# Handing a fused cross-attention kernel its context with the features on the partitions, and regrouping its PSUM banks

## The reference, cut to what matters

```python
# x: 16 batches of 128 tokens x 512 features; ctx_1024: 16 x 2048 x 512
# cross-attention with 16 query heads of 32 and ONE key/value head of 32
K, V = ctx @ Wk + bk, ctx @ Wv + bv                      # 2048 x 32 each
x = x + softmax((layernorm(x) @ Wq + bq) K^T / sqrt(32)) V @ Wo + bo
x = x + memory_attention(layernorm(x))                   # 4 heads of 128, a triangular inverse per head
x = x + moe(layernorm(x))                                # 16 experts, one per token, 128 tokens each
```

## Time and profile before

| what | value |
|---|---|
| time, median of 3 runs | 2176.65 us (2176.55 to 2177.91) |
| span of the profiled execution, first to last instruction | 2171.3 us |
| around the span, against the median | 5.35 us |
| PE busy, over the span | 2095.7 us (97%) |
| PE weight loads busy | 1421.6 us (65%) |
| POOL busy | 1635.7 us (75%) |
| DVE busy / ACT busy | 1272.3 us (59%) / 1220.7 us (56%) |
| transposes at L412 from the context in w_first | 992, mean 276 ns, together 151.5 us |
| mean granted TensorE clock | 0.986 |

### The profile page before, as it was taken

One profiled execution on the slowest core, in us unless ns is written; L12 is line 12 of the kernel. 1 busy time (PEld: TensorE's weight loads), 2 busy tenths in 40 slices (PEclk: granted clock), 3 DMA queues, 4 the chain that ended last, 5 costly groups with the idle time before them and its releaser, 6 DMA issues. The chain is left out here.

```text
span 2171.3 us, 35745 instructions
## 1 busy us (share of the span) xinstructions
PE 2095.7 (97%) x12908; PEld 1421.6 (65%) x12908; DVE 1272.3 (59%) x2226; ACT 1220.7 (56%) x2277; POOL 1635.7 (75%) x1387
## 2 busy tenths in 40 slices
PE   7879999999999999999999999999989999999999
PEld 5436565656565656666565656565645789999998
DVE  5656767676666666676767676766664433333332
ACT  3756575666666566666665666666655233433333
POOL 0778888888888888888888888889798145555555
PEclk8989999999999999999999999999999999999999
DMA  4752121212212121212131212112200089999994
GB/s 159 242 113 90 48 74 45 73 52 66 75 48 74 45 73 53 74 44 82 39 97 43 74 43 74 59 57 71 79 15 11 12 313 357 363 352 359 360 348 177
DMA packets 107055, 262.31 MB, mean 121 GB/s; under 512 B 8960, under 2 KB 34304, under 8 KB 98688
## 3 DMA queue, kind: packets, MB, share of 16 engines
q1 hardware_dynamic: 96912, 234.92, 31.6%
q10 hardware_dynamic: 6384, 14.62, 2.3%
q0 software_dynamic: 3584, 10.49, 1.2%
HBM read 223.67 MB, written 25.72 MB: 115 GB/s over the span
## 5 line engine op out<-in xcount | busy, mean ns | idle before, releaser
L1094 POOL TENSOR_TENSOR psum<-psum,weights 128x512 f32<-128x512 f32 x896 | 1152.6, 1286 | 163.4 <-ACT weights L702 60.5
L880 DVE TENSOR_REDUCE mpart<-bank 128x1 f32<-128x512 f32 x1024 | 680.4, 684 | 308.9 <-PE bank L447 300.0
L702 ACT ACTIVATE weights<-bank 128x512 f32<-128x512 f32 x1024 | 597.0, 599 | 324.1 <-PE bank L460 313.3
L460 PE MATMUL bank<-qT,kT 97*128 97x512 f32 x1024 | 482.8, 477 | 10.0 <-DMA qT<-mrow 6.5
L447 PE MATMUL bank<-kT,qT 96*128 96x512 f32 x1024 | 450.0, 451 | 9.6 <-DVE mpart L880 6.8
L447 PEld LDWEIGHTS bank<-kT,qT 96*128 96x128 f32 x1024 | 196.9, 192 | 141.2 <-issue 87.4
L1346 POOL TENSOR_TENSOR w2l<-w,w2h 128x1024 fp32r<-128x1024 f32 x64 | 202.9, 3171 | 75.8 <-PE ebank L1259 54.5
L460 PEld LDWEIGHTS bank<-qT,kT 97*128 97x128 f32 x1024 | 195.7, 193 | 89.4 <-issue 49.2
L472 PE MATMUL bank<-weights,v 128*32 128x512 f32 x2048 | 251.3, 609 | 0.0
L737 ACT COPY w_first<-bank 128x512 f32<-128x512 f32 x248 | 144.7, 584 | 67.6 <-PE bank L412 64.6
L1289 ACT ACTIVATE hh<-ebank 128x512 fp32r<-128x512 f32 x64 | 38.2, 597 | 224.6 <-PE ebank L1243 224.6
(11 more groups left out here) (174 smaller groups left out, 3019.3 us busy)
## 6 DMA issues: line engine op xcount, KB each, us to landing
w<-in_w SPq DMA_DIRECT2D x48, 2048.0 KB, 19.9
w_first<-in_ctx SPq DMA_DIRECT2D x62, 1024.0 KB, 5.2
w_first<-in_w SPq DMA_DIRECT2D x16, 2048.0 KB, 12.2
dispatched<-route ACTq DMA_DIRECT2D x17, 513.0 KB, 8.5
dis<-dispatched SPq DMA_DIRECT2D x16, 513.0 KB, 3.5
qT<-qh SPq DMA_DIRECT2D x128, 64.0 KB, 3.4
qT<-qs SPq DMA_DIRECT2D x64, 64.0 KB, 2.1
xr<-in_x SPq DMA_DIRECT2D x16, 256.0 KB, 2.7
```

Of the source, the lines that this page charges most:

```text
L460: e.matmul(B_BANK[u % 2][:], kT[b % 2][0:3 * HD + 1, k * P:(k + 1) * P], qT[b % 2][0:3 * HD + 1, g * 512:(g + 1) * 512], start=True, stop= ...
L702: e.activation(p[n % NP], B_BANK[u % 2][:], ACT.Exp).then_inc(p_act.sem, 1)
L880: e.tensor_reduce(mpart[g % 2][:, 4 * (n % 4) + n // 4:4 * (n % 4) + n // 4 + 1], max_bank(b, g, n)[:], AX.X, ALU.max).then_inc(max_dve.se ...
L1094: e.tensor_tensor(acc[:], first, p[(UNITS * b + u) % NP], ALU.add).then_inc(psum_pool.sem, 1)
```

## The change

The host now lays the context out as [batch, part, feature within a plane, plane, token], so that each part lands in SBUF as `kv` wants it. The 16 tile transposes of each batch, the copies behind them (ACT's, and DVE's for batch 0) and their waits are gone. All four parts of `cxT` have a place of their own, and the part of the batch after next is loaded four ticks after the `kv` step that frees its place. The bank `T_BANK` becomes the third bank of maxima; the turned `x` and the turned values go to `KV_BANK`. The other weights (`Wq`, `Wo` and so on) are laid out by planes too, which makes each partition's piece of a load contiguous. Preparation of batch 0 is pulled together.

```diff
-WARM = {-1: 14, 14: 4}
+WARM = {-1: 14, 10: 4}
...
-Prep = namedtuple("Prep", "norm xn xnt qproj qsend tiles kv vt")
-STEADY = Prep(norm=-32, xn=-29, xnt=-27, qproj=[24, 26, 27, 29], qsend=52,
-              tiles=[9, 12, 13, 15, 18, 24, 27, 32, 35, 39, 44, 50, 53, 54, 60, 69],
-              kv=[18, 37, 58, 74], vt=[42, 79])
+STEADY = Prep(norm=-32, xn=-29, xnt=-27, qproj=[24, 26, 27, 29], qsend=52, kv=[18, 37, 58, 74], vt=[42, 79])
...
-FIRST = Prep(norm=6, xn=9, xnt=12, qproj=[14, 15, 16, 17], qsend=22,
-             tiles=[2, 3, 4, 5, 6, 7, 8, 9, 19, 20, 21, 22, 28, 29, 30, 31], kv=[10, 23, 33, 38], vt=[27, 43])
-LOAD_AT = [13, 45, 71, 80]
+FIRST = Prep(norm=4, xn=6, xnt=8, qproj=[11, 12, 13, 14], qsend=19, kv=[7, 10, 16, 18], vt=[20, 22])
+LOAD_AFTER, W1_AT = 4, 80
...
-FIRST_MAX, FIRST_TURN = [35, 35, 36, 36, 40, 40, 41, 41, 42, 42, 43, 43, 44, 44, 45, 45], 47
+FIRST_MAX, FIRST_TURN = [24 + n // 2 for n in range(KB)], 33
...
-        A_BANK, B_BANK, PV_BANK, T_BANK, KV_BANK, P_BANK = bank[0:2], bank[2:4], bank[4], bank[5], bank[6], bank[7]
+        A_BANK, B_BANK, PV_BANK, KV_BANK, P_BANK = [bank[0], bank[1], bank[5]], bank[2:4], bank[4], bank[6], bank[7]
...
+            + [(TICKS * (b - 1) + prep(b).xnt, b, ("x", 0)) for b in range(B)]
+            + [(TICKS * (b - 1) + t, b, ("v", m)) for b in range(B) for m, t in enumerate(prep(b).vt)]
...
-            return [*A_BANK, P_BANK][n % 3] if b == g == 0 else A_BANK[(17 * g + n) % 2]
+            return A_BANK[(17 * (HG * b + g) + n) % 3]
+
+        def max_read(b, g, n):
+
+            before_g, before_n = divmod(17 * (HG * b + g) + n - 3, 17)
+            if before_g < 0:
+                return None
+            return max_dve.at(0, KB * before_g + before_n) if before_n < KB else mrow_act.at(0, before_g)
...
-                e.dma_start(chunk(b, c), T["ctx"][b].rearrange("(p c k) d -> c p k d", c=4, k=4)[c]).then_inc(
-                    ctx_in[c].sem, 16)
+                if b:
+                    e.wait_ge(*kv_pe.at(b - 1, c))
+                e.dma_start(cxT[c], T["ctx"][b, c]).then_inc(ctx_in[c].sem, 16)
...
-                if t in prep(b).tiles:
-                    k = prep(b).tiles.index(t)
-                    c, kk = divmod(k, 4)
-                    if kk == 0:
-                        e.wait_ge(*ctx_in[c].at(b))
-                    read = turn_read(b, ("t", k))
-                    if read is not None:
-                        e.wait_ge(*read)
-                    transposes(turn_bank(b, ("t", k)), lambda j: chunk(b, c)[:, kk, j * P:(j + 1) * P]).then_inc(t_pe.sem, 1)
                 if t in prep(b).kv:
                     c = prep(b).kv.index(t)
-                    e.wait_ge(*copied(b, 4 * c + 3))
+                    e.wait_ge(*ctx_in[c].at(b))
...
+    ctx = np.ascontiguousarray(g["ctx_1024"].reshape(B, 4, S // 4, DC, P).transpose(0, 1, 4, 3, 2))
```

More of the change, by code:

```diff
@@ L152, in attention @@
         pad_dve, pad_pool = sb("pad_dve", [P, 1]), sb("pad_pool", [P, 1])
-        cx = [w1_first[:, c, :].rearrange("p (k d) -> p k d", k=4) for c in range(2)]
-        cxT = [w1_first[:, 2 + c, :].rearrange("p (c t) -> p c t", c=DC) for c in range(2)]
-        def chunk(b, c):
-            return weights[:, 2048 * (c - 2):2048 * (c - 1)].rearrange("p (k d) -> p k d", k=4) if b == 0 and c >= 2 else cx[c % 2]
+        cxT = [w1_first[:, c, :].rearrange("p (c t) -> p c t", c=DC) for c in range(4)]
         kvlow, kvs = sb("kvlow", [P, 512]), [sb(f"kvs{i}", [P, 512]) for i in range(2)]
@@ L237, in level @@
             return (b, lv) if b < LAST else (b, 4 * lv + part)
-        uses = sorted((TICKS * b + t, b, use) for b in range(B) for t, use in
-                      [(prep(b).xnt, ("x", 0))] + [(t, ("t", k)) for k, t in enumerate(prep(b).tiles)]
-                      + [(t, ("v", c)) for c, t in enumerate(prep(b).vt)])
-        turns, holds, first_uses = {}, {}, 0
-        for _, b, use in uses:
-            place = 0
-            if b == 0:
-                place, first_uses = first_uses % 4, first_uses + 1
-            turns[b, use] = place, holds.get(place)
-            holds[place] = b, use
-        def copied(b, k):
-            if b:
-                return cxT_act.at(b, k - KB // 2)
-            return cxT_dve.at(0, k // 2) if k % 2 else cxT_act.at(0, k // 2)
-        def turn_bank(b, use):
-            return [T_BANK, *B_BANK, PV_BANK][turns[b, use][0]]
-        def turn_read(b, use):
-            if turns[b, use][1] is None:
-                return None
-            before_b, (kind, i) = turns[b, use][1]
-            if kind == "x":
-                return xnT_act.at(before_b)
-            return copied(before_b, i) if kind == "t" else v_act.at(before_b, i)
         kv_uses = [(b, use) for _, b, use in sorted(
@@ L311, in banks_of @@
         def banks_of(b):
-            return [P_BANK] if b < LAST else [P_BANK, KV_BANK, T_BANK, PV_BANK]
+            return [P_BANK] if b < LAST else [P_BANK, KV_BANK, A_BANK[2], PV_BANK]
         def att_done(b, h):
@@ L499, in prepare @@
                     e.wait_ge(*xn_act.at(b))
-                    read = turn_read(b, ("x", 0))
+                    read = kv_read(b, ("x", 0))
                     if read is not None:
                         e.wait_ge(*read)
-                    transposes(turn_bank(b, ("x", 0)), lambda j: xin[:, j * P:(j + 1) * P]).then_inc(xnT_pe.sem, 1)
+                    transposes(KV_BANK, lambda j: xin[:, j * P:(j + 1) * P]).then_inc(xnT_pe.sem, 1)
                 if t in prep(b).qproj:
@@ L537, in prepare @@
                         rows = slice(64 * (j % 2), 64 * (j % 2) + 2 * HD)
-                        ins = e.matmul(KV_BANK[rows, :], wkv[:, j, :], cxT[c % 2][:, j, :], start=j < 2, stop=j >= 2)
+                        ins = e.matmul(KV_BANK[rows, :], wkv[:, j, :], cxT[c][:, j, :], start=j < 2, stop=j >= 2)
                     ins.then_inc(kv_pe.sem, 1)
@@ L542, in prepare @@
                     e.wait_ge(*kvs_dve.at(b, 2 * m + 1))
-                    e.wait_ge(*turn_read(b, ("v", m)))
-                    transposes(turn_bank(b, ("v", m)), lambda j: kvs[m][:, j * P:(j + 1) * P]).then_inc(vT_pe.sem, 1)
+                    e.wait_ge(*kv_read(b, ("v", m)))
+                    transposes(KV_BANK, lambda j: kvs[m][:, j * P:(j + 1) * P]).then_inc(vT_pe.sem, 1)
             def finish(b, t):
@@ L724, in prepare @@
                     e.wait_ge(*xnT_pe.at(b))
-                    e.copy(xnT[:].rearrange("p c t -> p (c t)"), turn_bank(b, ("x", 0))[:]).then_inc(xnT_act.sem, 1)
+                    e.copy(xnT[:].rearrange("p c t -> p (c t)"), KV_BANK[:]).then_inc(xnT_act.sem, 1)
                 if t == prep(b).qproj[3] + 2:
```

74 lines of the change are left out of this document (23 added, 51 removed).

## The result

| | before | after |
|---|---|---|
| time, median | 2177.28 us (2176.55 to 2178.03, 4 runs) | 2141.61 us (2140.20 to 2145.51, 4 runs) |
| ratio, 95% interval | | 0.984 (0.9828 to 0.9853) |
| profiled execution: span | 2171.3 us | 2140.6 us (time 2142.43 us) |
| granted clock, whole span | 0.986 | 0.979 |

The change makes the kernel 35.7 us faster, 1.6%. So the time of before moves by some 4 us from one comparison to the next, and the gain is 31 to 36 us. In every run for which both numbers are known, the time is 1.8 to 1.9 us longer than the span of the same execution (here 2142.43 against 2140.6).

A forecast was written before the change was run, and what follows sets the result against it. POOL's in-order work was taken to bound C and A, the level chain B. Terms 1.2 + 1.55 + 0.4 - 0.25 = 2.9 us a batch, 14 times 40.6, plus 5 for pass 0: 45.6 less, 2131.0 us; range 2095 to 2152.

The forecast's parts named there:

- case 1: POOL and the chains take over: 2.0 to 4.2 us gained per batch, 2108 to 2149 us in all; chance 0.68.
- What bounds the kernel: Steady batches: POOL's slack is 1.3 us and 0.7 us at its meetings with PE; its idle time lies in B.
- B: Rest of the batch after `XT` is turned, 29.5 us: the chain of levels limits, gain 0.4 us per batch.
- A: From the sums to PE's turning of `XT`, 38.3 us: POOL's work limits the gain to 1.55 us, not 4.1.
- C: From POOL's restart after waiting for ACT to the next batch's sums: 33.4 us instead of 34.6, gain 1.2.
- Where PE waits: In A, PE's new idle time: 2 to 3 us at ticks 26 to 28, the rest at the turning of `XT`.
- The clock: Steady batches: PE's idle time may drop the granted clock, costing 0.25 us per batch, between 0 and two 1.6 us stretches.
- case 3: One stretch at half clock per batch, in A, eats part of the gain: 2153 us; chance 0.10.
- case 4: Half clock twice a batch, in A and among the levels, makes it slower: about 2182 us; chance 0.04.
- Pass 0: First pass: PE gets 7.2 us and more earlier to a maxima row stuck behind the zeros; gain 5 us, between 2 and 10.
- Start: Before the maxima: queries' projection starts near 21.5 instead of 18.7 us; net 0, between 3 us lost and 3 won.
- Pass 15: Last pass, which has no preparation of a next batch: no gain or loss, 0 us.

The follow-up runs named there:

- `after_again`: The changed kernel without any edit, run again on another chip beside its own runs of before: 2142.04 us, ratio 0.9857.
- run 1: Changed kernel with three of GpSimd's additions a batch (`xb`, `x12`, the queries' low part) moved to VectorE: 2121.13 us, ratio 0.9762.
- run 4: Changed kernel with two maxima banks, plus 16 groups of four identity transposes a batch without copy, wait or reader: 2169.53 us, ratio 0.9989.
- run 7: Also `rn_early`: changed kernel with only GpSimd's inverse norm `rn` moved from tick 33 to 32: 2137.76 us, ratio 0.9835.
- run 3: Changed kernel with two maxima banks, and `x` and the values turned in the freed bank instead of the keys' bank: 2138.97 us, ratio 0.9857.
- run 5: Changed kernel with the first keys' step two ticks later, the queries' first part one later, `rn` one earlier: 2174.17 us, ratio 1.0007.
- run 6: Changed kernel with three of GpSimd's additions on VectorE and the first keys' step two ticks later: 2149.57 us, ratio 0.9892.
- run 8: Changed kernel with its 17 writes of zeros every 10 ticks instead of 4, on into pass 1: 2132.99 us, ratio 0.9819.
- run 9: Kernel before the change, with its zeros written every 10 ticks: 2171.09 us, ratio 0.9985.

## Why the prediction was right, and where it was off

The forecast was 2131.0 us in a range of 2095 to 2152; measured were 2141.6 us. Sign and case are right (case 1: POOL and the chains take over); the sum is 10 us too large by medians (35.7 against 45.6), 14.9 us by the profiled spans (30.7), and 12.4 us by the span of `after_again` (33.2). The time came as near to the forecast as it did in part by luck: the 5.35 us that the forecast put around the span are 1.8 in the measured runs, and the rest of them, 3.5 us, is how much faster than its median the profiled execution of before was. By its own steps:

- *What bounds the kernel.* Right. GpSimd has the slack of 4 us in B, none in A, and in C only the 0.3 us before VectorE's statistics. Runs 1, 4 and 7 show it from three sides: 3.84 us less for GpSimd in A shorten A by 1.4 us; 7.2 us of TensorE's work brought back cost 1.7; a wait of TensorE of 1.2 us taken away gives 0.1. That the rest of the 3.84 us didn't come says how near the second limit is: TensorE and VectorE had about 1.4 us to spare in A.
- *C, gain 1.2.* GpSimd's 33.3 us stayed; the sums now follow after 0.40 us instead of 1.3, so 0.9.
- *A, gain 1.55, not 4.1.* The floor was 36.65 us of GpSimd's work, and A became 36.97 us for GpSimd without a wait in it. Measured by PE, 659.10 to 696.19, it is 37.1 instead of 38.3: 1.2. The term is mis-sized by 0.3 us, and the row says how: each of the twenty additions in A takes 1307 ns where it took 1295 before, 0.24 us in all.
- *Where PE waits.* Wrong in the place. I expected 2 to 3 us at ticks 26 to 28; there are 0.23 us there. The idle time (36.97 - 34.23 = 2.7 us in A) stands before the keys (tick 18) and the turning of `rk` (tick 42). I had named the shared keys' bank as free "in the steady state"; a step does meet it, yet run 3 shows that this costs nothing, and run 5 that the step standing there even covers a worse wait.
- *B, gain 0.4.* Right in size: 29.1 us for PE (696.19 to 725.3) against 29.5. Level 1's products are 2.19 us apart, not 1.94. At the first two products of the levels the distance did go from 2.14 to 1.94 us. So the space of the tile group was given back there, and the sign named for level 1 was wrong.
- *The clock, -0.25.* Zero: the granted clock is 1.00 from 200 to 1500 us. Cases 3 and 4 are out for this change. The waits of up to 1.22 us were not followed by a fall; in run 5 one of 2.75 us was followed by 0.50. The rule of the Trainium skill that case 3 named (TensorE: Matmul & The Clock Gate, HAM oscillation) did not come into play in the steady batches of the changed kernel. In run 5 the trace agrees with it in all twelve batches, and in run 6 in seven of twelve, behind the same wait. Case 3 said that the trace of before bears it out in pass 15 only; the clock of 0.61 around the wait of pass 0 bears it out as well.
- *The batch.* C 0.9, A 1.2 and B 0.4 make 2.5; measured 2.4. Pass 1 alone gave 0.5, since GpSimd there waits 2.48 us for DVE's second statistics. So 31.5 us in 14 passes instead of 40.6 (33.4 in `after_again`, where pass 1 gave 1.9). This is the largest part of what is missing: 2.4 instead of 2.9 us a batch, and the terms of A and C are the ones that were too large.
- *Pass 0, +5.* By the first profile 0.2 us, by `after_again` 3.9 (the first addition of pass 1 at 157.78 and 154.06, against 157.97 in the one profile of before). The term said that TensorE gets there 7.2 us earlier and the DMA queue gives way by some of it. How much it gives way by differs that much between two executions of one kernel, so the term is not refuted, but no single profile can size it. What it had wrong is the place: TensorE stood at the third group too (8.85 and 6.72 us), a wait that before did not have. Runs 8 and 9 settle that it is the zeros: with them spread the same removal is worth 7.2 us.
- *Start, 0.* 0.8 us lost (first scores at 50.56 against 49.73), inside the three either way; the projection of the queries stood at 22.18, predicted 21.5.
- *Pass 15, 0.* 1.0 us lost: 94.55 us from its first addition to the end of the last, against 93.6, with GpSimd's first wait for DVE's statistics at 1.35 us instead of 0.39. But the kernel before with spread zeros, whose pass 15 is the same code as that of before, takes 95.0 us, and `rn_early` 93.2. So executions differ by as much, and no loss is shown.
- *Experts, 0.* 487.5 us from the last addition of pass 15 to the end, in both first profiles. In `after_again` it is 490.4 and across all runs 487.1 to 490.8, though no edit touches this part: another 3 us by which a time can differ.

Missing from the sum of 45.6, by the first profiles: 9.1 us in the batches, 4.8 in what ends with pass 0, 1.0 in pass 15; this is the whole of 14.9. By `after_again`: 7.2 in the batches, 1.1 up to the end of pass 0, 1.1 in pass 15 and 3.0 in the experts. In both the batches are the largest part.

## What to carry to other kernels

Look for the meeting points of the in-order engines and cut the period there: an engine at 98% can be worth a quarter of what is taken from it, when another one works without a gap in just those stretches. A wait that stands in front of a step may be the cover of the next, so move a step only after asking what its place hides; an idle time of TensorE that grew from 1.13 to 2.75 us was paid twice here, with 1.3 us by itself and with 1.6 by the clock wherever that fell behind it. Small rows that carry a dependence belong in time ahead of bulk writes, even of writes on another queue.
